# First attention of a two-layer block: key tiles taken two at a time, in phases, on TensorE

## The chip, the cores and the metric

One Trainium2 chip, one of its cores. The number is the device time of one execution in microseconds (us), the median of several. Five engines of the core work at once, each through its own list of instructions, in order, and wait for one another by semaphores: TensorE (PE, matrix products; its weight loads are listed apart as PEld), VectorE (DVE), ScalarE (ACT), GpSimd (POOL), and SyncE (SP), which here only issues DMAs.

## What is computed

Sequence of 2048 tokens of 128 features, two layers; each sub-layer is followed by a residual addition and a layer norm. The change touches the first sub-layer alone, causal attention with 16 heads of 64:

```python
q = jnp.einsum('bpm,hmd->bphd', x, Q_w) + Q_b          # k, v alike
logits = jnp.einsum('bqhd,bkhd->bhqk', q, k) / math.sqrt(D_HEAD)
logits = jnp.where(causal, NEG_MASK, logits)            # keys after the query
scores = jax.nn.softmax(logits, axis=-1)
attn = jnp.einsum('bhqk,bkhd->bqhd', scores, v)
return jnp.einsum('bqhd,hdm->bqm', attn, O_w) + O_b
```

Behind it come a gated feed-forward network, a second attention with 16 heads of 8, and a linear layer. They are the same in both kernels.

## The kernel before

**Units and turns.** Two heads are worked together, one in partitions 0 to 63, one in 64 to 127. A unit `u` is one such pair of heads (`p`, eight of them) and one block of 512 queries (`qc`, four of them), 32 units in all. A turn is one unit and one tile of 128 keys (`kt`); a unit has 4, 8, 12 or 16 turns, a pair of heads 40, the whole 320. The last four turns of a unit lie on the diagonal: they compute 512, 384, 256 and 128 queries (512, 512, 256 and 128 in a unit with `qc` 0).

**A turn on TensorE.** `scores` makes the transposed logits of both heads in `ps_e` (two slots of two banks, by the parity of the turn): three products per head of float16 parts (line 491, 64 rows of the array each, the two heads in the two halves of it), on the diagonal a mask product on 128 rows (L496, L497), and a product with two rows that subtracts the row maximum (`maxima`, L512). The maxima of an even turn come last in its slot; those of the odd turn behind it are issued right behind them as the first write of the other slot, so that the four stand together. ScalarE takes the exponential (`exps`, L383) into one of six buffers `probs`; TensorE multiplies it with the values into `ps_o` (`pv`, L527, float32, each head in 64 columns of the array); GpSimd adds the same buffers up to the row sums (L348, L353).

**Maximum blocks.** The row maxima are needed ahead of a unit. For later units, some 20 turns ahead, TensorE makes the logits of 128 queries against up to 512 keys in `ps_x`, one slot of two banks (`max_block`, L443, on 64 rows; a block on the diagonal gets a mask product, L447, on 128 rows), and VectorE reduces them (`take_max`, L592). The next block waits until that reduction is done (`s_xf`). There are 320 blocks, nearly always one per turn, in the order `u`, `t` (query tile), `c` (block of keys). Behind a unit's last block VectorE joins its parts and splits them into two bfloat16 rows (`split_max`, L601 to L605), TensorE transposes them (`mt`, L456), and SyncE copies them with four small DMAs to `mrow`, for which the unit's maxima wait (`s_mrd`).

**Ring work.** One bank `ps_y` serves, at most once per turn, at the turn's end and strictly in order, the operations that `plan` lays out: projections of q and k of the next pair of heads (`qk`, L425; ScalarE empties the bank with L400, then VectorE with L619), its values (`v`, L429; ScalarE, L407), and for each finished unit the sum over partitions (`sum`, L465; VectorE, L623), its spread (`bc`, L470; VectorE, L627) and the output projection (`yo`, L472; VectorE, L635). Each waits until the one before it has been emptied (`s_yf`). 208 of 320 turns have one.

**Order.** TensorE per turn: `scores`, first maximum block, `pv` of the turn before, other maximum blocks, ring operation. VectorE per turn: reduction of the blocks, then its part of the ring operation. ScalarE per turn: exponential, at a unit's first turn the copy of `ps_o` of the unit before (L390), its part of the ring operation. A turn's products wait for the exponential of two turns before (`s_ex`), and the first turn of a unit for `s_mrd` ahead of its products.

Of the kernel before, what the change touches and what calls it, by code (L numbers as in the profile page):

```python
# [14 lines left out]
P = 128  # L15
# [4 lines left out]
NQ = S // QC  # L20
H0, D0 = 16, 64
# [119 lines left out]
def build(nc, a, out):  # L141
# [10 lines left out]
    with ExitStack() as ctx:  # L152
# [82 lines left out]
        def diag(qc, kt):  # L235
            return kt - 4 * qc if kt >= 4 * qc else None

        def off(qc, kt):

            j = diag(qc, kt)  # L240
            return 0 if j is None or kt < 2 else P * j

        BLOCKS = [(u, t, c) for u in range(NU) for t in range(4) for c in range(u % NQ + 1)]
# [113 lines left out]
        def _(act):  # L357
# [52 lines left out]
            for turn, (u, kt) in enumerate(TURNS):  # L410
                exps(turn)
                if kt == 0 and u > 0:
                    copy_pv(u - 1)
                for op in PLAN[turn][1]:
                    empty(op)
# [3 lines left out]
        def _(pe):  # L419
# [13 lines left out]
            def max_block(n, b):  # L433
                u, t, c = BLOCKS[b]
                p, qc = divmod(u, NQ)
                w = width(b)
                if n:
                    pe.wait_ge(s_xf, n)
                if p > 0 and b == BEND[u - 1] and qc == 0:
                    pe.wait_ge(s_yf, AT["qk", 8 * p + 7] + 1)  # L440
                for h in range(2):
                    rows = slice(D0 * h, D0 * h + D0)
                    mm = pe.matmul(ps_x[:, h, 0:w], hi["q"][rows, p % 2, (4 * qc + t) * P:(4 * qc + t + 1) * P],  # L443
                                   hi["k"][rows, p % 2, c * QC:c * QC + w], start=True, stop=c < qc)
                if c == qc:
                    for h in range(2):
                        mm = pe.matmul(ps_x[:, h, w - P:w], identb[:, :], mask[:, :], start=False, stop=True)  # L447
                mm.then_inc(s_xp, 1)
# [26 lines left out]
            def scores(turn):  # L475
                u, kt = TURNS[turn]
                p, qc = divmod(u, NQ)
                o = off(qc, kt)
                keys = slice(kt * P, (kt + 1) * P)
                queries = slice(qc * QC + o, (qc + 1) * QC)  # L480
                out = ps_e[:, turn % 2]
                j = diag(qc, kt)
                if kt == 0:
                    pe.wait_ge(s_mrd[u % 4], 64 * (u // 4 + 1))
                if turn >= 2 and turn % 2 == 0:
                    pe.wait_ge(s_ex, turn - 1)
                products = ((hi, hi), (hi, lo), (lo, hi))
                for n, (k_part, q_part) in enumerate(products):
                    for h in range(2):
                        rows = slice(D0 * h, D0 * h + D0)  # L490
                        mm = pe.matmul(out[:, h, o:], k_part["k"][rows, p % 2, keys], q_part["q"][rows, p % 2, queries],  # L491
                                       start=n == 0 and turn % 2 == 0, stop=n == 2 and j is None and turn % 2 == 1)
                if j is not None:
                    for h in range(2):
                        for b in range(o // P, j):
                            pe.matmul(out[:, h, b * P:(b + 1) * P], allneg[:, :], identb[:, :], start=False, stop=False)  # L496
                        mm = pe.matmul(out[:, h, j * P:(j + 1) * P], mask[:, :], identb[:, :], start=False,  # L497
                                       stop=turn % 2 == 1)
                if turn % 2 == 0:
                    mm = maxima(turn, 0)  # L500
                mm.then_inc(s_st, 1)
                if turn % 2 == 0:
                    if turn >= 1:
                        pe.wait_ge(s_ex, turn)
                    maxima(turn + 1, 1)

            def maxima(turn, first):
                u, kt = TURNS[turn]
                o = off(u % NQ, kt)
                for h in range(2):  # L510
                    row = 64 * h + 32 * first
                    mm = pe.matmul(ps_e[:, turn % 2, h, o:], negone[row:row + 2, :], mrow[row:row + 2, u % 4, o:],  # L512
                                   start=first == 1, stop=first == 0)
                return mm
# [38 lines left out]
            for b in range(BEND[0]):  # L553
                max_block(b, b)
# [4 lines left out]
            for turn, (xs, ys) in enumerate(PLAN):  # L559
                scores(turn)  # L560
                for b in xs[:1]:
                    max_block(b, b)
                if turn > 0:
                    pv(turn - 1)
                for b in xs[1:]:
                    max_block(b, b)
                for op in ys:
                    use_y(op)
# [5 lines left out]
        def _(dve):  # L574
# [71 lines left out]
            for xs, ys in PLAN:  # L646
                for b in xs:
                    take_max(b, b)
                for op in ys:
                    empty(op)  # L650
# [875 lines left out]
```

## Time and profile before

| | us |
|---|---|
| median of 3 runs | 2081.2 (2079.88 to 2084.37) |
| profiled execution, time | 2082.02 |
| its span in the trace | 2080.3 |
| first attention, turns 0 to 319 and tail | from 36 to 952 |
| TensorE granted clock, mean | 0.933 |

The profile is of one execution; times in it count from the start of the span. An engine is busy while one of its instructions is in flight. TensorE's products are pipelined, so what one costs is read as the distance from its start to the start of the next, and not from its duration, which contains the time through the array. "PEclk" is the granted TensorE clock as a share of 2.4 GHz; 0.50 is the lower of its two levels, 1.2 GHz.

### The profile page before, as it was taken

The page shows a single profiled execution, that of the slowest core. Times are in us where ns is not written, and L with a number is a line of the kernel's source. Part 1 is how long each engine was busy: PE and PEld are TensorE (multiplying, and loading weights), DVE is VectorE, ACT ScalarE, POOL GpSimd, SP SyncE. Part 2 cuts the span into 40 slices and gives each one's busy share as a digit, 9 for nine tenths or more (in the row PEclk, how much of TensorE's full clock was granted, in tenths as well). Part 3 has the DMA queues.
Part 4 walks back from the last instruction along what each step waited for, and adds up shares of the span by engine and source line. Part 5 has one row for each costly group of instructions (what it writes and reads, how often), then busy time and mean ns, then how long its engine had stood idle before and what let it go on. Part 6 is the DMA issues. An engine that isn't in the chain of part 4 may idle for free. (4 is left out here: it accounts for less than half of the span.)

```text
span 2080.3 us, 27643 instructions
## 1 busy us (share of the span) xinstructions
PE 1738.2 (84%) x11088; PEld 559.5 (27%) x11088; DVE 1288.8 (62%) x1810; ACT 940.1 (45%) x1087; POOL 596.3 (29%) x313
## 2 busy tenths in 40 slices
PE   5889999999999999994999503788888888888873
PEld 2233333333333333323444300111111111111111
DVE  3545555564655555524200785888888888888816
ACT  2334443444434444341311300477777777677760
POOL 0357576757575756681000300000000000000000
PEclk8899999999999999995999755799999999999996
DMA  3000000000000000001000145011110021110000
GB/s 61 1 1 1 1 1 1 2 1 2 1 1 1 2 1 1 1 1 56 0 0 0 17 171 98 1 21 40 35 21 20 20 43 32 21 20 20 2 3 23
DMA packets 47714, 39.03 MB, mean 19 GB/s; under 512 B 19519, under 2 KB 42595, under 8 KB 47587
## 3 DMA queue, kind: packets, MB, share of 16 engines
q1 hardware_dynamic: 41394, 35.71, 7.6%
q10 hardware_dynamic: 6192, 1.57, 0.5%
q8 instruction: 87, 1.43, 0.3%
q14 instruction: 41, 0.33, 0.0%
HBM read 25.53 MB, written 10.49 MB: 17 GB/s over the span
## 5 line engine op out<-in xcount | busy, mean ns | idle before, releaser
L1214 ACT ACTIVATE probs<-ps_e 128x1024 f32<-128x1024 f32 x512 | 498.1, 1022 | 256.9 <-PE ps_e L1275 256.8
L353 POOL TENSOR_TENSOR acc<-acc,probs 128x1024 f32<-128x1024 f32 (+3 forms) x256 | 502.2, 1962 | 174.4 <-ACT probs L383 161.7
L592 DVE TENSOR_REDUCE maxpart<-ps_x 128x2 f32<-128x1024 f32 (+2 forms) x320 | 340.4, 1064 | 240.9 <-PE ps_x L447 121.5
L383 ACT ACTIVATE probs<-ps_e 128x1024 f32<-128x1024 f32 (+1 forms) x320 | 288.6, 902 | 426.5 <-PE ps_e L512 257.5
L1335 DVE TENSOR_REDUCE maxpart<-ps_x 128x2 f32<-128x1024 f32 x351 | 428.1, 1220 | 66.8 <-PE ps_x L1239 64.0
L527 PE MATMUL ps_o<-probs,v 128*64 128x512 f32 (+3 forms) x1280 | 309.0, 561 | 0.6 <-ACT pv_raw L390 0.6
L1285 PE MATMUL ps_o<-probs,v 128*9 128x512 f32 x2048 | 269.2, 598 | 46.5 <-ACT probs L1214 30.8
L1239 PE MATMUL ps_x<-krows,qrows 60*128 60x512 bf16 x702 | 152.7, 402 | 144.3 <-DMA qrows<-g_rows 72.2
L1339 DVE TENSOR_REDUCE maxpart<-ps_y 128x1 f32<-128x512 f32 x322 | 220.4, 685 | 18.8 <-PE ps_y L1239 15.9
L1275 PE MATMUL ps_e<-qrows,krows 62*128 62x512 bf16 x1024 | 220.6, 384 | 7.4 <-DMA qrows<-maxrow 3.7
L1239 PE MATMUL ps_y<-krows,qrows 60*128 60x512 bf16 x322 | 129.2, 401 | 7.8
L443 PE MATMUL ps_x<-k_hi,q_hi 64*128 64x512 f16 (+3 forms) x640 | 116.7, 361 | 18.6 <-DVE maxpart L592 16.9
L348 POOL TENSOR_TENSOR acc<-probs 128x1024 f32<-128x1024 f32 x32 | 75.1, 2348 | 190.2 <-ACT probs L383 190.2
L491 PE MATMUL ps_e<-q_hi,k_hi 64*128 64x512 f16 (+3 forms) x640 | 116.1, 360 | 10.7 <-DMA mrow<-maxrow 10.7
L1239 PEld LDWEIGHTS ps_x<-krows,qrows 60*128 60x128 bf16 x702 | 36.2, 94 | 302.9 <-DVE maxpart L1335 212.9
L491 PE MATMUL ps_e<-q_lo,k_hi 64*128 64x512 f16 (+3 forms) x640 | 112.8, 349 | 0.0
L491 PE MATMUL ps_e<-q_hi,k_lo 64*128 64x512 f16 (+3 forms) x640 | 112.7, 349 | 0.0
L1275 PEld LDWEIGHTS ps_e<-qrows,krows 62*128 62x128 bf16 x1024 | 58.9, 95 | 101.1 <-ACT probs L1214 73.0
L527 PEld LDWEIGHTS ps_o<-probs,v 128*64 128x64 f32 x1280 | 63.7, 135 | 64.7 <-issue 50.4
L791 DVE SCALAR_TENSOR_TENSOR yt<-ps_f,sc_w,xt 128x512 f32<-128x512 f32 x4 | 3.0, 751 | 121.7 <-PE ps_f L748 121.7
L491 PEld LDWEIGHTS ps_e<-q_hi,k_hi 64*128 64x128 f16 x640 | 30.8, 93 | 166.8 <-issue 119.8
L1239 PEld LDWEIGHTS ps_y<-krows,qrows 60*128 60x128 bf16 x322 | 30.5, 95 | 134.2 <-DVE maxpart L1339 105.5
(222 smaller groups left out, 1531.0 us busy)
## 6 DMA issues: line engine op xcount, KB each, us to landing
qrows<-q_rows SPq DMA_DIRECT2D x64, 192.0 KB
k_rows<-parts_k SPq DMA_DIRECT2D x6, 512.0 KB
q_rows<-parts_q SPq DMA_DIRECT2D x6, 512.0 KB
krows<-k_rows SPq DMA_DIRECT2D x8, 384.0 KB, 7.2
qrows<-g_rows SPq DMA_DIRECT2D x64, 48.0 KB
mrow<-maxrow SPq DMA_DIRECT2D x128, 2.0 KB
raw_h<-in_L_ffn_h_w SPq DMA_DIRECT2D x2, 1024.0 KB, 7.1
g_rows<-parts_a SPq DMA_DIRECT2D x6, 256.0 KB
```

What stands on the lines that cost most here:

```text
L353: pool.tensor_tensor(acc[:, u % 2, :, o:], acc[:, u % 2, :, o:], probs[:, turn % RING, :, o:], ALU.add)\
L383: act.activation(probs[:, turn % RING, :, o:], ps_e[:, turn % 2, :, o:], ACT.Exp, scale=1.0 / math.sqrt(D0))\
L443: mm = pe.matmul(ps_x[:, h, 0:w], hi["q"][rows, p % 2, (4 * qc + t) * P:(4 * qc + t + 1) * P], hi["k"][rows, p % 2, c * QC:c * QC + w], st ...
L491: mm = pe.matmul(out[:, h, o:], k_part["k"][rows, p % 2, keys], q_part["q"][rows, p % 2, queries], start=n == 0 and turn % 2 == 0, stop=n ...
L527: mm = pe.matmul(ps_o[D0 * h:D0 * h + D0, o:], v[:, p % 2, kt, D0 * h:D0 * h + D0], probs[:, turn % RING, h, o:], start=kt == 0, stop=kt = ...
L592: dve.reduce_max(maxpart[:, u % 2, :, t, c:c + 1], ps_x[:, :, 0:width(b)], AX.X).then_inc(s_xf, 1)
L1214: act.activation(probs[:, HG * (turn % 2) + hh], ps_e[:, e % 2], ACT.Exp).then_inc(s_ex, 1)
L1239: return pe.matmul(out, qrows[64 * j:64 * j + R_M, u % 3, c, hh, t * P:(t + 1) * P], krows[64 * j:64 * j + R_M, u // NQ % 2, hh, c * KB:(c ...
L1275: mm = pe.matmul(ps_e[:, e % 2, j], krows[64 * j:64 * j + R_END, u // NQ % 2, hh, at * P:(at + 1) * P], qrows[64 * j:64 * j + R_END, u % 3 ...
L1285: mm = pe.matmul(ps_o[32 * hh:32 * hh + D1 + 1, :], v1[:, TU * j + at, HG * (u // NQ) + hh, :], probs[:, HG * (turn % 2) + hh, j, :], star ...
L1335: dve.reduce_max(maxpart[:, at:at + op[2]], ps_x[:, 0:op[2], :], AX.X).then_inc(s_xf, 1)
L1339: dve.reduce_max(maxpart[:, at:at + 1], ps_y[:, :], AX.X).then_inc(s_yf, 1)
```

## The change

Two turns are taken together. TensorE: first maximum block of the two (with its mask), products of both turns, products of the second maximum block, masks of both turns, mask of the second block, maxima of both turns, `pv` of the turn two before, any further blocks and the first turn's ring operation, then `pv` of the turn one before and the second turn's ring operation. ScalarE: both exponentials, then the copy of `ps_o`, then both ring parts. VectorE: the reductions of both turns' blocks, then both ring parts. The order of the blocks within a unit now alternates a full block with a diagonal one as long as there are diagonal ones. The wait for `s_mrd` stands ahead of the maxima, no longer ahead of the products. Numbers and sizes of all instructions stay the same; GpSimd and SyncE are as they were.

```diff
--- before.py
+++ after.py
@@ -240,7 +240,15 @@
             j = diag(qc, kt)
             return 0 if j is None or kt < 2 else P * j
 
-        BLOCKS = [(u, t, c) for u in range(NU) for t in range(4) for c in range(u % NQ + 1)]
+        def unit_blocks(u):
+
+            qc = u % NQ
+            full = [(u, t, c) for t in range(4) for c in range(qc)]
+            last = [(u, t, qc) for t in range(4)]
+            mixed = [b for two in zip(full, last) for b in two]
+            return mixed + full[4:] if full else last
+
+        BLOCKS = [b for u in range(NU) for b in unit_blocks(u)]
         BEND = [sum(4 * (w % NQ + 1) for w in range(u + 1)) for u in range(NU)]
 
         def width(b):
@@ -407,12 +415,15 @@
                     act.activation(v[:, p % 2, 4 * g:4 * g + 4, :].rearrange("p t d -> p (t d)"), ps_y[:, :], ACT.Copy)\
                         .then_inc(s_yf, 1)
 
-            for turn, (u, kt) in enumerate(TURNS):
+            for turn in range(0, len(TURNS), 2):
+                u, kt = TURNS[turn]
                 exps(turn)
+                exps(turn + 1)
                 if kt == 0 and u > 0:
                     copy_pv(u - 1)
-                for op in PLAN[turn][1]:
-                    empty(op)
+                for t in (turn, turn + 1):
+                    for op in PLAN[t][1]:
+                        empty(op)
             copy_pv(NU - 1)
 
         @block.tensor
@@ -430,22 +441,32 @@
                                    wv[:, 2 * p:2 * p + 2, :].rearrange("m h d -> m (h d)"), start=True, stop=True)
                 return mm
 
-            def max_block(n, b):
+            def max_products(b):
                 u, t, c = BLOCKS[b]
                 p, qc = divmod(u, NQ)
                 w = width(b)
-                if n:
-                    pe.wait_ge(s_xf, n)
+                if b:
+                    pe.wait_ge(s_xf, b)
                 if p > 0 and b == BEND[u - 1] and qc == 0:
                     pe.wait_ge(s_yf, AT["qk", 8 * p + 7] + 1)
                 for h in range(2):
                     rows = slice(D0 * h, D0 * h + D0)
                     mm = pe.matmul(ps_x[:, h, 0:w], hi["q"][rows, p % 2, (4 * qc + t) * P:(4 * qc + t + 1) * P],
                                    hi["k"][rows, p % 2, c * QC:c * QC + w], start=True, stop=c < qc)
-                if c == qc:
+                if c < qc:
+                    mm.then_inc(s_xp, 1)
+
+            def max_mask(b):
+                u, t, c = BLOCKS[b]
+                w = width(b)
+                if c == u % NQ:
                     for h in range(2):
                         mm = pe.matmul(ps_x[:, h, w - P:w], identb[:, :], mask[:, :], start=False, stop=True)
-                mm.then_inc(s_xp, 1)
+                    mm.then_inc(s_xp, 1)
+
+            def max_block(b):
+                max_products(b)
+                max_mask(b)
 
             def use_y(op):
                 kind, i, n = op
@@ -472,46 +493,40 @@
-            def scores(turn):
+            def products(turn):
                 u, kt = TURNS[turn]
                 p, qc = divmod(u, NQ)
                 o = off(qc, kt)
                 keys = slice(kt * P, (kt + 1) * P)
                 queries = slice(qc * QC + o, (qc + 1) * QC)
-                out = ps_e[:, turn % 2]
-                j = diag(qc, kt)
+                if turn >= 2:
+                    pe.wait_ge(s_ex, turn - 1)
+                for n, (k_part, q_part) in enumerate(((hi, hi), (hi, lo), (lo, hi))):
+                    for h in range(2):
+                        rows = slice(D0 * h, D0 * h + D0)
+                        pe.matmul(ps_e[:, turn % 2, h, o:], k_part["k"][rows, p % 2, keys],
+                                  q_part["q"][rows, p % 2, queries], start=n == 0, stop=False)
+
+            def score_masks(turn):
+                u, kt = TURNS[turn]
+                o, j = off(u % NQ, kt), diag(u % NQ, kt)
+                if j is not None:
+                    for h in range(2):
+                        out = ps_e[:, turn % 2, h]
+                        for b in range(o // P, j):
+                            pe.matmul(out[:, b * P:(b + 1) * P], allneg[:, :], identb[:, :], start=False, stop=False)
+                        pe.matmul(out[:, j * P:(j + 1) * P], mask[:, :], identb[:, :], start=False, stop=False)
+
+            def maxima(turn):
+                u, kt = TURNS[turn]
+                o = off(u % NQ, kt)
                 if kt == 0:
                     pe.wait_ge(s_mrd[u % 4], 64 * (u // 4 + 1))
-                if turn >= 2 and turn % 2 == 0:
-                    pe.wait_ge(s_ex, turn - 1)
-                products = ((hi, hi), (hi, lo), (lo, hi))
-                for n, (k_part, q_part) in enumerate(products):
-                    for h in range(2):
-                        rows = slice(D0 * h, D0 * h + D0)
-                        mm = pe.matmul(out[:, h, o:], k_part["k"][rows, p % 2, keys], q_part["q"][rows, p % 2, queries],
-                                       start=n == 0 and turn % 2 == 0, stop=n == 2 and j is None and turn % 2 == 1)
-                if j is not None:
-                    for h in range(2):
-                        for b in range(o // P, j):
-                            pe.matmul(out[:, h, b * P:(b + 1) * P], allneg[:, :], identb[:, :], start=False, stop=False)
-                        mm = pe.matmul(out[:, h, j * P:(j + 1) * P], mask[:, :], identb[:, :], start=False,
-                                       stop=turn % 2 == 1)
-                if turn % 2 == 0:
-                    mm = maxima(turn, 0)
+                for h in range(2):
+                    row = 64 * h + 32 * (turn % 2)
+                    mm = pe.matmul(ps_e[:, turn % 2, h, o:], negone[row:row + 2, :], mrow[row:row + 2, u % 4, o:],
+                                   start=False, stop=True)
                 mm.then_inc(s_st, 1)
-                if turn % 2 == 0:
-                    if turn >= 1:
-                        pe.wait_ge(s_ex, turn)
-                    maxima(turn + 1, 1)
-
-            def maxima(turn, first):
-                u, kt = TURNS[turn]
-                o = off(u % NQ, kt)
-                for h in range(2):
-                    row = 64 * h + 32 * first
-                    mm = pe.matmul(ps_e[:, turn % 2, h, o:], negone[row:row + 2, :], mrow[row:row + 2, u % 4, o:],
-                                   start=first == 1, stop=first == 0)
-                return mm
 
             def pv(turn):
                 u, kt = TURNS[turn]
@@ -551,21 +566,35 @@
             pe.wait_ge(s_cst, 12)
             pe.wait_ge(s_cstv, 1)
             for b in range(BEND[0]):
-                max_block(b, b)
+                max_block(b)
             for op in BEFORE:
                 use_y(op)
             pe.wait_ge(s_pjv, 4)
             pe.wait_ge(s_ob, 2)
-            for turn, (xs, ys) in enumerate(PLAN):
-                scores(turn)
+            for turn in range(0, len(TURNS), 2):
+                two = (turn, turn + 1)
+                xs = [b for t in two for b in PLAN[t][0]]
                 for b in xs[:1]:
-                    max_block(b, b)
-                if turn > 0:
-                    pv(turn - 1)
-                for b in xs[1:]:
-                    max_block(b, b)
-                for op in ys:
-                    use_y(op)
+                    max_block(b)
+                for t in two:
+                    products(t)
+                for b in xs[1:2]:
+                    max_products(b)
+                for t in two:
+                    score_masks(t)
+                for b in xs[1:2]:
+                    max_mask(b)
+                for t in two:
+                    maxima(t)
+                for t in two:
+                    if turn > 0:
+                        pv(t - 2)
+                    if t == turn:
+                        for b in xs[2:]:
+                            max_block(b)
+                    for op in PLAN[t][1]:
+                        use_y(op)
+            pv(len(TURNS) - 2)
             pv(len(TURNS) - 1)
             for op in AFTER:
                 use_y(op)
@@ -643,11 +672,13 @@
             dve.wait_ge(s_ob, 2)
             dve.wait_ge(s_xtc, 4)
             dve.tensor_scalar(yt[:, :], xt[:, :], obias[:, 0:1], None, ALU.add).then_inc(s_yi, 1)
-            for xs, ys in PLAN:
+            for turn in range(0, len(TURNS), 2):
+                xs = [b for t in (turn, turn + 1) for b in PLAN[t][0]]
                 for b in xs:
                     take_max(b, b)
-                for op in ys:
-                    empty(op)
+                for t in (turn, turn + 1):
+                    for op in PLAN[t][1]:
+                        empty(op)
             for op in AFTER:
                 empty(op)
             dve.wait_ge(s_yf, len(AT))
```

## Rows read from the trace of the kernel before

**Rows 1.** The page's first part, busy time of each engine

```profile
PE 1738.2 (84%) x11088; PEld 559.5 (27%) x11088; DVE 1288.8 (62%) x1810; ACT 940.1 (45%) x1087; POOL 596.3 (29%) x313
```

**Rows 2.** Windows: stretch, length, busy us by engine, granted clock, DMA share, GB/s

```profile
36.00:147.00 111.00, 90.09 (x533) 29.97 (x533) 56.41 (x70) 30.25 (x38) 40.09 (x21) 0.82 0.00 1
705.00:816.00 111.00, 110.69 (x784) 38.92 (x782) 62.55 (x77) 45.93 (x57) 72.16 (x36) 1.00 0.01 1
1500.00:1900.00 400.00, 331.86 (x2360) 72.74 (x2356) 355.96 (x433) 284.99 (x298) 0.00 (x0) 1.00 0.13 27
```

**Rows 3.** Timeline, VectorE: one event in three successive pairs of heads

```profile
499.86 1.59 DVE L603 CAST maxhl<-rowmax 128x8 bf16<-128x8 f32 x1
...
610.65 1.59 DVE L603 CAST maxhl<-rowmax 128x8 bf16<-128x8 f32 x1
...
721.43 1.59 DVE L603 CAST maxhl<-rowmax 128x8 bf16<-128x8 f32 x1
```

**Rows 4.** Timeline, TensorE, from 703.40: start, duration, engine, line, out<-in, count

```profile
703.40 0.39 PE L491 MATMUL ps_e<-q_hi,k_hi 64*128 64x512 f16 x2
...
704.15 0.39 PE L512 MATMUL ps_e<-mrow,negone 2*128 2x512 bf16 x4
704.48 0.39 PE L443 MATMUL ps_x<-k_hi,q_hi 64*128 64x512 f16 x2
704.80 1.08 PE L527 MATMUL ps_o<-probs,v 128*64 128x512 f32 x4
705.81 0.39 PE L491 MATMUL ps_e<-q_hi,k_hi 64*128 64x512 f16 x2
...
706.47 0.27 PE L443 MATMUL ps_x<-k_hi,q_hi 64*128 64x256 f16 x2
706.67 0.28 PE L447 MATMUL ps_x<-mask,identb 128*128 128x128 bf16 x2
706.89 1.08 PE L527 MATMUL ps_o<-probs,v 128*64 128x512 f32 x4
707.90 0.64 PE L465 MATMUL ps_y<-acc,ones 128*32 128x128 f32 x16
708.48 0.39 PE L491 MATMUL ps_e<-q_hi,k_hi 64*128 64x512 f16 x2
```

**Rows 5.** Timeline, VectorE: a reciprocal behind the sum at 707.90

```profile
708.61 0.96 DVE L623 RECIPROCAL rden<-ps_y 128x128 f32<-128x128 f32 x1 [0.92 <-PE ps_y L465]
```

**Rows 6.** Timeline, 723 to 725: a block that waited for VectorE

```profile
723.14 1.22 DVE L592 TENSOR_REDUCE maxpart<-ps_x 128x2 f32<-128x1024 f32 x1
724.42 0.39 PE L443 MATMUL ps_x<-k_hi,q_hi 64*128 64x512 f16 x2
724.85 1.23 DVE L592 TENSOR_REDUCE maxpart<-ps_x 128x2 f32<-128x1024 f32 x1 [0.37 <-PE ps_x L443]
```

**Rows 7.** Timeline, 641 to 645: a projection and what empties it

```profile
641.99 1.12 PE L425 MATMUL ps_y<-xt,wq 128*128 128x512 f32 x2
643.05 0.39 PE L491 MATMUL ps_e<-q_hi,k_hi 64*128 64x512 f16 x2
643.16 0.69 ACT L400 ACTIVATE q_hi<-ps_y,bq 128x512 f16<-128x512 f32 x1 [1.48 <-PE ps_y L425]
643.88 0.75 DVE L619 SCALAR_TENSOR_TENSOR q_lo<-ps_y,bq,q_hi 128x512 f16<-128x512 f32 x1 [1.55 <-ACT q_hi L400]
644.57 1.23 DVE L592 TENSOR_REDUCE maxpart<-ps_x 128x2 f32<-128x1024 f32 x1
```

**Rows 8.** Groups by line and form: count, busy us, mean ns, idle before

```profile
L383 ACT ACTIVATE probs<-ps_e 128x1024 f32<-128x1024 f32 x232 | 237.7, 1025 | 335.9 <-PE ps_e L512 223.4 <-PE ps_e L491 100.8 <-PE ps_e L497 9.6
L353 POOL TENSOR_TENSOR acc<-acc,probs 128x1024 f32<-128x1024 f32 x168 | 395.0, 2351 | 118.6 <-ACT probs L383 111.4 <-POOL acc L353 0.4
L627 DVE TENSOR_TENSOR ctxn<-pv_raw,ps_y 128x512 f32<-128x512 f32 x32 | 22.0, 688 | 29.2 <-PE ps_y L470 29.2
L390 ACT ACTIVATE pv_raw<-ps_o 128x512 f32<-128x512 f32 x32 | 18.9, 592 | 0.7 <-PE ps_o L527 0.7
```

**Rows 9.** Timeline, TensorE: the two waits for mrow ahead of clock drops

```profile
60.72 0.39 PE L491 MATMUL ps_e<-q_hi,k_hi 64*128 64x512 f16 x2 [1.78 <-DMA mrow<-maxrow]
63.91 0.64 PE L491 MATMUL ps_e<-q_hi,k_hi 64*128 64x512 f16 x2
136.47 0.39 PE L491 MATMUL ps_e<-q_hi,k_hi 64*128 64x512 f16 x2 [2.86 <-DMA mrow<-maxrow]
```

**Rows 10.** Windows around the second of those waits

```profile
137.00:147.00 10.00, 6.84 (x38) 3.23 (x34) 5.04 (x8) 1.62 (x2) 0.00 (x0) 0.52 0.01 2
```


## The prediction

> **What bounds the kernel now.** I read the page's first part, then windows over the attention, then TensorE's timeline in it. Over the span TensorE is in flight 84% of the time [rows 1]; in the attention it is in flight 110.69 of 111 us at a granted clock of 1.00, VectorE 62.55, ScalarE 45.93, GpSimd 72.16 [rows 2]. So TensorE's issue sets the time from about 147 us on, and each microsecond taken from its stream, or in which it waits, shows in the end. The first 111 us are different: 90.09 in flight, clock 0.82. A pair of heads, 40 turns, repeats every 110.8 us (one event recurs at 499.86, 610.65 and 721.43) [rows 3].
>
> The timeline gives each group's price as distance between starts [rows 4]. Products of a turn: 0.66 if another group on 64 rows follows (705.81 to 706.47), 0.75 if one on two rows follows (703.40 to 704.15). The four maxima to the block 0.33, a full block to `pv` 0.32; at 512 columns one pass of two halves is 0.66/3 = 0.22. A block of 256 to its mask 0.20, the mask's pair to `pv` 0.22, `pv` 1.01, the sum 0.58. In each place where the use of the array changes (64 rows, two rows, 128 rows, 64 columns) about 0.10 is paid: 0.75 - 0.66, 0.33 - 0.22, 0.32 - 0.22.
>
> **What the change takes away.** No instruction is removed; their neighbours change. From the two orders in the code I counted the places per 40 turns where the use of the array changes: 188 before, 122 after. Behind a `pv` there were 40 of them and are 34: 6 of the 66 lie there, where another `pv` follows, a neighbourhood that these rows do not show. Its price is between 4 x 0.22 = 0.87 (no seam at all) and 1.01 (nothing saved); I take 0.96, that of two halves, and the bounds are worth 0.5 us per 40 turns. So TensorE's stream loses 60 x 0.10 + 6 x 0.05 = 6.3, and goes from 110.8 less 0.6 of waits to 103.9 us per 40 turns.
>
> The Trainium skill (TensorEngine Tiling, Key Properties) says that changing the tiling mode drains the engine; by it all 66 places would save alike, 6.6 in place of 6.3. The same page (PSUM Bottleneck) says that tiling speeds TensorE up and not the emptying of PSUM: a rule against this change. The next part finds the same from rows.
>
> **What it adds: waits for VectorE.** A pair of turns now begins with a block X0, then come two turns of products, then a second block X1 in the same single slot `ps_x`. X1 waits for the reduction of X0, and all of TensorE behind it. In the before a `pv` (1.01) and a turn's products (0.66, or 0.75 and 0.33 of maxima) lay between two blocks, 2.0 us from start to start or more. Price of the loop: block start to reduction start 0.43 (724.42 to 724.85), the full reduction 1.23, and 0.06 from its end to the next block (723.14 + 1.22 = 724.36, block at 724.42) [rows 6]: 1.72. Cover now: X0 0.22 and two products of 0.66, 1.54. So even the undisturbed pair waits 0.18. Where the turns are 512 and 384 wide the cover is 0.16 shorter, wait 0.34; at 256 and 128 (0.34 and 0.18 in place of 1.32) it is 0.98.
>
> Worse: VectorE takes its work in order, and in front of X0's reduction lies its part of the ring operation that TensorE issued just before X0. Before, that had a whole turn's products as cover.
> - `qk`: TensorE start 641.99, next group at 643.05, ScalarE 643.16 to 643.85, VectorE from 643.88, and the reduction queued behind it starts at 644.57 [rows 7], 1.52 after the next group. Now X0 is that next group: reduction done at 1.52 + 1.23 + 0.06 = 2.81 against a cover of 1.54: wait 1.26.
> - `sum`: issued at 707.90, next group 708.48 [rows 4], reciprocal from 708.61 for 0.96, to 709.57 [rows 5]. The reduction starts about 1.0 after X0 in place of 0.43: wait 0.74.
> - `bc` and `yo`: TensorE's group is some 1.07 long, VectorE needs 0.69 behind it [rows 8]: 0.30 later than free, wait 0.48.
> - `v` has no VectorE part: 0.18 again.
>
> In the plan `qk` is due on odd turns, so 5 of 8 end a pair. I laid the changed order of 40 turns (120 to 159, units 12 to 15) on these prices, engine by engine. Of the 20 pairs 5 wait 0.18 (0.9), 1 waits 0.34, 1 0.98, 1 0.61 (a masked 384-wide X0 before narrow turns), 3 behind `sum` 0.74, 0.74 and 1.54 (narrow), 3 behind `bc` or `yo` 0.48, 5 behind `qk`: 1.26, 1.26, 1.42, 1.52 and, before narrow turns, 2.53. Together 0.9 + 1.9 + 3.0 + 1.4 + 8.0 = 15.2.
>
> **Ring operations closer together.** When both turns of a pair have one, only one `pv` lies between them. A `qk` in the even turn must be emptied by ScalarE, which now has two exponentials of 1.03 first and sometimes the copy of `ps_o` (0.59) [rows 8], then by VectorE. The second waits four times in these 40 turns: 2.16 (behind a 128-wide `pv`), 0.84, 0.63, 0.11, sum 3.7.
>
> Net per 40 turns: -6.3 - 0.6 (the old waits, among them) + 15.2 + 3.7 = +12.0 us.
>
> **Other edits.** Products wait for the exponential two turns before: two exponentials in a row need 2.1 us behind the maxima, and two `pv` (1.97), X0 and the first products (0.66) stand ahead of the second one's slot; cost nothing, at narrow `pv` at most 0.3 once per unit. If that cover went, it would cost 0.4 to 0.7 per pair. GpSimd's add takes 2.35 [rows 8], a pair of full turns some 5.5; six buffers hold that. SP's DMAs keep their work, and the `mrow` wait moves behind 1.3 us of products: it held TensorE 1.78 and 2.86 at 60.72 and 136.47 [rows 9], so 1 to 3 us come back in all.
>
> **The sum.** Against the profiled execution's 2082.0 (span 2080.3): turns 0 to 39, where few `qk` stand behind narrow turns and the `mrow` waits shrink, -2.5 (bounds -7 to +5: they are bound by blocks already); turns 40 to 279, six pairs of heads, 6 x 12.0 = +72; turns 280 to 319 have no `qk` and no `v` of a next pair, 7 to 8 of waits against 6 saved, +2. That is +71.5, 2153.5. The same laying of the old order gives 915 us for the attention where the trace has 916, so the prices are sound.
>
> **The clock.** After the `mrow` waits of 1.78 and 2.86 the granted clock fell to its lower level: products at 63.91 take 0.64 in place of 0.39, and 137 to 147 shows 0.52 [rows 9, 10]. Later, 1500 to 1900, TensorE is in flight 83% of the time and keeps 1.00 [rows 2]. The changed attention would be around 85%, but with single waits of 2.5 and 2.2 us once per 40 turns, near those that were followed by a fall. I expect some eight falls of 7 to 10 us in the attention that weren't there. All of the first 111 us, at 0.82, lose only 5 or 6 us against the same laying at full clock, since other waits hide it; so I take +1 per fall, +8, bounds 0 and 3.4 each (half of a 7 us stretch), 0 to 27. **2161** on the median, which is 0.8 below the profiled time.
>
> **Rivals.**
> - *The waits are covered* (other side): TensorE's X1 finds the reduction done, since VectorE's ring parts end early enough. It decides if a reduction is done within 1.54 of X0. Then 6.3 per 40 turns are left, 8 x 6.5 = 52: 2030. Against it: 1.72 is measured and is over 1.54 with nothing in front. 0.05.
> - *Half of it*: half the waits, as VectorE is less late than laid. Per 40 turns 0.5 x 18.9 - 6.9 = +2.6, 6 x 2.6 = +16: 2097. For it: the few waits of before for this slot were 0.2 each. 0.05. Down to no change at all: 0.02.
> - *The seams don't shrink*: 0.10 is paid for whatever follows, also between two products or two `pv`. Then 50 more, 2205. Against: 0.66 and 0.75 differ only by the neighbour. 0.04.
> - *The clock falls often*: each pair of heads has 3 or 4 falls at 2 to 3 us each, +60 more: 2200. For it: the 19 waits per 40 turns; against: 83% at 1.00 [rows 2]. 0.09. [...]
> - Forecast: the remaining 0.75.
>
> The range takes the forecast with its bounds (2161 less 27 for the size of waits and falls, with a fifth of the waits on either side, 6 x 3.8 = 23) and part of the two upper rivals: 2122 to 2195. A change under 0.2% (4 us) can't be told from none. Faster 0.05, same 0.02, slower 0.93.
>
> **What the profile after would show.** Right: in 40 turns, about 123 us in place of 110.8; PE or PEld idle before L443's counterpart, released by `maxpart`, 14 to 16 us per 40 turns, in single waits of 0.2 to 2.5; products to second block 1.32 plus the wait; `pv` behind maxima; waits of ring operations for ScalarE or VectorE; VectorE's busy time unchanged, with less idle per reduction waiting for TensorE's maxima; the attention ending near 1025 to 1030. Wrong: TensorE still in flight 99% of the attention; or idle before L443 under 5 us per 40 turns; or idle before the products, released by `probs`; or a clock under 0.9 over 200 to 900.

## The result and the profile after

The changed kernel takes 2167.3 us (2166.84 to 2169.73) against 2082.8 for the kernel before measured beside it: ratio 1.041, 95% interval 1.0392 to 1.0428, slower. Predicted were 2161 us and a range of 2122 to 2195. The profiled execution took 2167.78 us with a span of 2166.1.

The page's first part of the changed kernel, to be read against [rows 1]:

```profile
PE 1714.9 (79%) x11088; PEld 582.4 (27%) x11088; DVE 1308.0 (60%) x1810; ACT 921.7 (43%) x1087; POOL 596.0 (28%) x313
```

Same counts on every engine, but TensorE is in flight for a smaller share of a longer span. Windows of the changed kernel over the attention (columns as in [rows 2]):

```profile
36.00:147.00 111.00, 85.48 (x562) 31.87 (x558) 58.84 (x73) 32.05 (x42) 42.85 (x23) 0.88 0.00 1
250.00:850.00 600.00, 520.19 (x3767) 201.17 (x3764) 310.86 (x365) 206.66 (x268) 347.38 (x174) 0.97 0.01 1
```

520 of 600 us in flight, where the kernel before had 110.69 of 111, and a granted clock of 0.97 in place of 1.00: two losses. Of the first, the waits in the same window say what it is (waiting engine, line, released by: us in total, times, longest):

```profile
PEld ps_x L454 <- DVE maxpart L621: 99.0, 94, 2.5
...
PE ps_x L454 <- DVE maxpart L621: 59.1, 69, 2.3
```

L454 is the product of a maximum block, L621 VectorE's reduction. The weight load and the product of one wait are counted apart, so these are not to be added.

How often a pair of heads repeats is read from an event that recurs, as in [rows 3]:

```profile
376.97 2.31 DVE L632 CAST maxhl<-rowmax 128x8 bf16<-128x8 f32 x1
...
503.21 2.32 DVE L632 CAST maxhl<-rowmax 128x8 bf16<-128x8 f32 x1
...
629.34 2.31 DVE L632 CAST maxhl<-rowmax 128x8 bf16<-128x8 f32 x1
```

126.2 us against 110.8. In what follows "per 40 turns" is this period, or the distance from the products of turn 40 to those of turn 280, divided by six (126.5 in the changed kernel, since the first of the six periods is 1.7 longer). The span grew by 85.8, made up of: turns 40 to 279 +94.3 (759.0 against 664.7), the 40 before -2.0, the 38 behind -1.9, what lies ahead of the attention -2.8, what follows it -1.9.

The worst single wait, on the timeline: a projection (L436) stands in front of a pair of narrow turns. Some rows of ScalarE and VectorE between are kept:

```profile
437.42 1.12 PE L436 MATMUL ps_y<-xt,wk 128*128 128x512 f32 x2
438.47 0.39 PE L454 MATMUL ps_x<-k_hi,q_hi 64*128 64x512 f16 x2
438.55 0.61 ACT L398 ACTIVATE pv_raw<-ps_o 128x512 f32<-128x512 f32 x1
...
439.02 0.70 ACT L408 ACTIVATE k_hi<-ps_y,bk 128x512 f16<-128x512 f32 x1
...
439.14 0.22 PE L507 MATMUL ps_e<-q_hi,k_lo 64*128 64x128 f16 x2
439.75 0.75 DVE L648 SCALAR_TENSOR_TENSOR k_lo<-ps_y,bk,k_hi 128x512 f16<-128x512 f32 x1 [2.57 <-ACT k_hi L408]
440.42 1.22 DVE L621 TENSOR_REDUCE maxpart<-ps_x 128x2 f32<-128x1024 f32 x1
441.69 0.61 PE L454 MATMUL ps_x<-k_hi,q_hi 64*128 64x512 f16 x2 [2.34 <-DVE maxpart L621]
...
443.10 3.68 PE L542 MATMUL ps_o<-probs,v 128*64 128x512 f32 x8
```

X0 is issued at 438.47. Its reduction starts at 440.42, for VectorE first has to finish the projection, and that waits for ScalarE, which copies `ps_o` first. X1 gets through 0.05 after the reduction, at 441.69. And its product now takes 0.61 in place of 0.39: the granted clock has gone to its lower level, and two `pv` are in flight for 3.68. At full clock, earlier in the same kernel, two `pv` look like this:

```profile
427.60 1.94 PE L542 MATMUL ps_o<-probs,v 128*64 128x512 f32 x8
429.47 0.39 PE L454 MATMUL ps_x<-k_hi,q_hi 64*128 64x512 f16 x2
```

From start to start 1.87 for both, where 1.97 had been taken (0.96 and 1.01 [rows 4]). The merged line hides the second start; in the trace it comes 0.91 after the first, and the next group 0.96 after that.

### The profile page after: what moved, and what is told of

Its sections match the earlier page's. It is cut to its first block and busy times, and to the rows that moved or that the text cites. A ratio compares the mean times of both kernels' runs of the same rounds, so it can differ in the third digit from the quotient of the medians.

```text
span 2166.1 us, 27612 instructions
## 1 busy us (share of the span) xinstructions
PE 1714.9 (79%) x11088; PEld 582.4 (27%) x11088; DVE 1308.0 (60%) x1810; ACT 921.7 (43%) x1087; POOL 596.0 (28%) x313
## 5 line engine op out<-in xcount | busy, mean ns | idle before, releaser
L391 ACT ACTIVATE probs<-ps_e 128x1024 f32<-128x1024 f32 (+1 forms) x320 | 270.9, 898 | 565.0 <-PE ps_e L527 565.0
L621 DVE TENSOR_REDUCE maxpart<-ps_x 128x2 f32<-128x1024 f32 (+2 forms) x320 | 338.9, 1059 | 201.5 <-PE ps_x L464 106.5
L542 PE MATMUL ps_o<-probs,v 128*64 128x512 f32 (+3 forms) x1280 | 303.6, 568 | 0.0
L454 PE MATMUL ps_x<-k_hi,q_hi 64*128 64x512 f16 (+3 forms) x640 | 119.5, 370 | 103.9 <-DVE maxpart L621 102.6
L454 PEld LDWEIGHTS ps_x<-k_hi,q_hi 64*128 64x128 f16 x640 | 31.2, 94 | 250.6 <-DVE maxpart L621 175.6
L542 PEld LDWEIGHTS ps_o<-probs,v 128*64 128x64 f32 x1280 | 69.8, 138 | 100.0 <-issue 63.3
L652 DVE RECIPROCAL rden<-ps_y 128x128 f32<-128x128 f32 x32 | 30.6, 957 | 73.7 <-PE ps_y L486 73.7
```

Of the source, the lines that this page charges most:

```text
L391: act.activation(probs[:, turn % RING, :, o:], ps_e[:, turn % 2, :, o:], ACT.Exp, scale=1.0 / math.sqrt(D0))\
L542: mm = pe.matmul(ps_o[D0 * h:D0 * h + D0, o:], v[:, p % 2, kt, D0 * h:D0 * h + D0], probs[:, turn % RING, h, o:], start=kt == 0, stop=kt = ...
L621: dve.reduce_max(maxpart[:, u % 2, :, t, c:c + 1], ps_x[:, :, 0:width(b)], AX.X).then_inc(s_xf, 1)
```

## Experiments

Two theories to begin with. A: the loss is X1's wait for the reduction of X0 in the single slot `ps_x`, made longer by what stands in front of it on VectorE. B: the loss comes from ring operations that stand closer together and from the paired exponentials, and the blocks only show it.

**e1: the second block behind the first `pv`.**

```diff
-                for b in xs[1:2]:
-                    max_products(b)
                 for t in two:
                     score_masks(t)
-                for b in xs[1:2]:
-                    max_mask(b)
...
                     if turn > 0:
                         pv(t - 2)
                     if t == turn:
-                        for b in xs[2:]:
+                        for b in xs[1:]:
                             max_block(b)
```

> The changed kernel with one move: the second maximum block of a pair (products and mask) is issued behind the first pv, no longer behind the products. Between X0 and X1 there are then 0.22 + 1.32 + 0.33 + 0.86 = 2.7 us and more, over the 1.72 that the slot needs, at narrow turns about 1.6. Theory A (the time lost is X1's wait for the reduction of X0 in the one slot): waits before blocks fall from 15 us to about 4 per 40 turns, those of ring operations stay at 4 to 5, 40 turns take about 113 us in place of 126; total 2104, range 2092 to 2115. Theory B (the time is lost to ring operations that stand too close together and to the paired exponentials; blocks only show it): under 3 us per 40 turns change hands, total 2145 or more.

Measured: 2092.8 us, ratio 1.0048 (1.0031 to 1.0064); 40 turns take 112.5 us. Waits from 250 to 850 us, and under them one row of the changed kernel in the same window:

```profile
PE ps_y L493 <- DVE k_lo L644: 10.3, 5, 2.1
...
PE ps_x L454 <- DVE maxpart L617: 4.3, 10, 0.5
```

```profile
PE ps_y L493 <- DVE k_lo L648: 8.2, 4, 2.1
```

Products that waited for the slot: 59.1 us became 4.3. The wait of the output projection (L493) for a `k_lo` in front of it, 2.1 each, is still there, as it is in the changed kernel. Moving this one block gives back 75 of 85 us, at the lower end of A's range: A holds. The 75 hold more than the wait itself, since from turn 40 to 280 the clock fell twice in place of eleven times. What ring operations cost is the next experiment.

**e2: blocks and ring operations both spread over the pair.** On TensorE:

```diff
-                for b in xs[:1]:
-                    max_block(b)
                 for t in two:
                     products(t)
-                for b in xs[1:2]:
+                for b in xs[:1]:
                     max_products(b)
...
-                for b in xs[1:2]:
+                for b in xs[:1]:
                     max_mask(b)
+                for op in PLAN[turn][1]:
+                    use_y(op)
                 for t in two:
                     maxima(t)
-                for t in two:
...
+                if turn > 0:
+                    pv(turn - 2)
+                for b in xs[1:2]:
+                    max_block(b)
+                if turn > 0:
+                    pv(turn - 1)
+                for b in xs[2:]:
+                    max_block(b)
+                for op in PLAN[turn + 1][1]:
+                    use_y(op)
```

ScalarE empties the first ring operation ahead of both exponentials; VectorE takes block, ring part, block, ring part.

> Blocks and ring operations both spread over the pair: TensorE does products of both turns, first block, masks, first ring operation, maxima, first pv, second block, second pv, second ring operation; ScalarE empties the first ring operation ahead of the two exponentials; VectorE takes block, ring, block, ring. Theory A, with ring operations as second term: 40 turns take about 107 us (before 110.8, changed 126.2), no single wait over 1.7 us from turn 40 on and so no falls of the clock there; total 2046, range 2038 to 2056, faster than both. Theory B (the paired exponentials or seams that aren't saved bound it): 2085 or more, with idle time before products released by probs.

Measured: 2042.1 us, ratio 0.9807 (0.9792 to 0.9822), inside A's range, faster than the kernel before by 41 us and than the changed one by 125; 40 turns take 106.7 us, and the clock did not fall between turns 40 and 280. Window and waits:

```profile
250.00:850.00 600.00, 594.83 (x4430) 226.31 (x4430) 340.59 (x425) 240.94 (x312) 408.39 (x205) 1.00 0.01 1
```

```profile
PEld ps_x L455 <- DVE maxpart L624: 47.1, 59, 1.2
...
PE ps_x L455 <- DVE maxpart L624: 4.7, 16, 0.4
...
PE ps_e L508 <- ACT probs L391: 0.3, 1, 0.3
```

The 47 us of the weight load are hidden under products in flight (TensorE is in flight 594.83 of 600); products waited 4.7 us. The paired exponentials cost 0.3 us in 600. So B falls as the main cause; what it says of ring operations is the second term: e1 takes 112.0 in a period without a fall, 5.3 more than e2, at nearly the same number of changes of use. Pairing turns does save TensorE time, but e2 has other neighbours than the changed kernel. Counted in the traces, turns 120 to 159, the use of the array changes 187 times in the kernel before, 122 times in the changed one, 146 times in e2 and 148 times in e1. The 41 fewer of e2 (187 less 146) at 0.10 are 4.1 us, and 110.8 less 106.7 is 4.1.

**e3: the changed kernel with short reductions.**

```diff
-                dve.reduce_max(maxpart[:, u % 2, :, t, c:c + 1], ps_x[:, :, 0:width(b)], AX.X).then_inc(s_xf, 1)
+                dve.reduce_max(maxpart[:, u % 2, :, t, c:c + 1], ps_x[:, :, 0:P], AX.X).then_inc(s_xf, 1)
```

> The changed kernel, but VectorE's reduction of a block reads the first 128 of its columns only (the maxima over the other keys are left out); 0.43 us in place of up to 1.23. TensorE's stream is the same. Theory A: waits before blocks fall from 15 to about 4 us per 40 turns (what is left is VectorE's ring part queued in front), 40 turns take 112 us plus some 4 for the clock; total 2087, range 2078 to 2098. Theory B: waits of ring operations and of the clock stay and the time stays over 2140.

Measured: 2063.9 us; 112.6 us per 40 turns. Waits from 250 to 850 us:

```profile
PE ps_x L454 <- DVE maxpart L621: 17.6, 30, 1.5
PE ps_y L493 <- DVE k_lo L648: 10.3, 5, 2.1
```

The direction is A's, and so is the wait before blocks, 59.1 down to 17.6. The total is below A's range by 14: most of the 4 us per 40 turns set aside for the clock were not needed, although the clock fell once in each of the six periods, for 3.4 us.

**e4: the changed kernel with the projections one turn later.**

```diff
-                    due.setdefault(TP * (p - 1) + 1 + 2 * i, []).append(("qk", 8 * p + i))
+                    due.setdefault(TP * (p - 1) + 2 + 2 * i, []).append(("qk", 8 * p + i))
```

> The changed kernel, with the projections of q and k due one turn later, on even turns, so that a pv lies between most of them and the next first block. Waits per 40 turns: 16 in place of 19, and the single waits over 1.7 us behind turn 40 go from 13 to 1. If the falls of the clock come from the longest single waits, they go too, and with them 20 to 24 us: total 2131, range 2122 to 2145. If the falls come from the sum of waits, they stay: 2150 to 2160.

Measured: 2144.1 us, 120.8 per 40 turns, at the upper end of the first range. Window and waits of 250 to 850:

```profile
250.00:850.00 600.00, 530.68 (x3902) 203.91 (x3902) 323.37 (x377) 215.96 (x277) 358.43 (x179) 1.00 0.01 1
```

```profile
PEld ps_x L454 <- DVE maxpart L621: 90.8, 105, 1.6
...
PE ps_x L454 <- DVE maxpart L621: 46.7, 70, 1.3
```

The sum of waits at weight loads is nearly that of the changed kernel (90.8 against 99.0), at products it is 46.7 against 59.1. The longest before a block is 1.6 in place of 2.5. No product waited over 1.4 for anything, and no fall of the clock is left: 1.00. This speaks for long single waits as what brings the lower clock here, and against their sum, which the second expectation named.

**e5 and e6: waits put into the kernel before.** Does one long wait do it anywhere?

```diff
+                for n_ in range(3 if u % NQ == 3 and t == 2 and c == 0 else 0):
+                    dve.reduce_max(spare[:, n_, :], ps_x[:, :, 0:width(b)], AX.X)
                 dve.reduce_max(maxpart[:, u % 2, :, t, c:c + 1], ps_x[:, :, 0:width(b)], AX.X).then_inc(s_xf, 1)
```

e6 has one repetition, ahead of each of four blocks (`c == 0`).

> The kernel before, with three idle repetitions of one reduction on VectorE (1.23 us each) ahead of one block per pair of heads, eight places in all. By the prices of the rows each makes TensorE wait 2.5 us there and 0.35 a little later, 21 to 23 us in all. Theory F1 (a single wait of 2.5 us brings the lower clock, wherever it stands): seven or eight falls behind turn 40, at 2 to 3 us each, total 2120 to 2125. Theory F2 (the fall needs other waits close by, as in the changed kernel; TensorE's stream of before is dense): none to two falls, total 2104 to 2106.

> The kernel before, with one idle repetition of a reduction (1.23 us) ahead of four blocks per pair of heads. By the prices one wait of 1.4 us and one of 0.4 per pair of heads, 14 us in all. Both theories: no fall of the clock behind turn 40; total 2097, range 2094 to 2101.

Measured: e5 2118.4 us, between its theories; 114.3 per 40 turns. Its wait of 2.54 stands once in each of the six periods between turns 40 and 280. The clock fell behind three of the six, every other one, for 3.4 us each. One of them, on TensorE's timeline:

```profile
460.29 0.39 PE L444 MATMUL ps_x<-k_hi,q_hi 64*128 64x512 f16 x2 [2.54 <-DVE maxpart L595]
460.61 1.08 PE L528 MATMUL ps_o<-probs,v 128*64 128x512 f32 x4
461.62 1.97 PE L473 MATMUL ps_y<-ctxn,wo 128*128 128x512 f32 x2
463.52 0.61 PE L492 MATMUL ps_e<-q_hi,k_hi 64*128 64x512 f16 x2
```

The output projection takes 1.90 in place of 1.06. e6, with single waits of at most 1.2 before the product, took 2100.7 us, in its range (112.9 per 40 turns), and had one fall between turns 40 and 280, where none was expected, at 202 us; the kernel before has none there. So a wait of 2.5 us was followed by a fall three times in six even in a dense stream, one of 1.2 once in six. Neither F1 nor F2 is right as stated. The total of e5 is 12 over F2's range: besides the falls, the turns before 40 took 6.3 us more than in the kernel before, and turns 280 to 318 took 7.2 more.

The length of a wait does not settle it alone. The changed kernel, e8 and e9 (below) have the same twelve long waits between turns 40 and 280, six of 2.3 and six of 2.1 us at a product, and eleven, five and three falls. e3 and e1 both have six of 2.1, and six and two falls. The sum does not settle it either: between turns 40 and 280 the products of e3 waited 42 us in all, with six falls, those of e4 83 us, with none. What else decides, no run here shows.

**e7: e2 with the old order of blocks.** `BLOCKS` as in the kernel before.

> The kernel e2 with the order of blocks within a unit as in the kernel before. The seams and the slot's distances stay nearly as they are: same time as e2, 2042, within 3 us. If alternating full with diagonal blocks is what made room for the slot, 2050 or more.

Measured: 2042.2 us, ratio 0.9806 (0.9789 to 0.9822), 106.7 us per 40 turns: the alternation of full and diagonal blocks does nothing in this arrangement. In the changed kernel itself it was not tried.

**e8 and e9: the cast of eight columns.** Comparing the changed kernel's pairs of turns with the laid order one by one, two per 40 turns were too long without a fall of the clock: turns 138 and 139 took 9.06 us where 7.8 had been laid, 152 and 153 5.38 for 4.6. In the first stands this (GpSimd, VectorE, TensorE):

```profile
503.15 4.84 POOL L361 TENSOR_TENSOR acc<-acc,probs 128x1024 f32<-128x1024 f32 x2 [2.37 <-ACT probs L391]
503.21 2.32 DVE L632 CAST maxhl<-rowmax 128x8 bf16<-128x8 f32 x1
...
505.64 0.68 DVE L656 TENSOR_TENSOR ctxn<-pv_raw,ps_y 128x512 f32<-128x512 f32 x1
506.38 1.12 PE L493 MATMUL ps_y<-ctxn,wo 128*128 128x512 f32 x2 [1.27 <-DVE ctxn L656]
```

The cast of eight columns starts 0.06 us after the first of two GpSimd adds, which the line merges, and ends with that add, 2.3 us later; TensorE waits 1.27 for what is queued behind it. In the kernel before, 14 of 32 casts began while a GpSimd add was running; all 14 took 1.56 to 1.59 [rows 3], the other 18 took 0.17. There it cost TensorE nothing: no wait of its products from turn 40 to 280 was over 0.1 us.

e8 gives GpSimd almost nothing to do:

```diff
-                    pool.tensor_tensor(acc[:, u % 2, :, o:], acc[:, u % 2, :, o:], probs[:, turn % RING, :, o:], ALU.add)\
+                    pool.tensor_tensor(acc[:, u % 2, :, o:o + 8], acc[:, u % 2, :, o:o + 8], probs[:, turn % RING, :, o:o + 8], ALU.add)\
```

> The changed kernel with GpSimd's adds of the third and later key tiles over 8 columns in place of up to 512 per head (most of the row sums is left out), so that GpSimd is nearly idle. Theory C (VectorE's cast of 8 columns, 2.3 us twice per pair of heads against 0.17 at best, is held for as long as a GpSimd add runs): every cast takes 0.17, pairs 138 and 152 of the timeline come down from 9.06 and 5.38 to 7.8 and 4.6 us, 40 turns from 126.2 to about 124, total 2154, range 2148 to 2160. If the cast is slow for another reason, the total stays at 2167.

e9 does without the cast:

```diff
-                dve.wait_ge(s_rm, 2 * u + 1)
-                dve.tensor_copy(maxhl[:, :, 0, :], rowmax[:, :, :]).then_inc(s_rm, 1)
+                dve.reduce_max(maxhl[:, :, 0, :], maxpart[:, u % 2, :, :, 0:u % NQ + 1], AX.X).then_inc(s_rm, 1)
```

> The changed kernel with the cast replaced by a second reduction straight into bfloat16. Theory C1 (GpSimd's add holds every small VectorE operation that reads a second SBUF input too): the wait moves to the subtraction behind it, which reads two, and that takes up to 2.3 us; total 2165 to 2169, as the changed kernel. Theory C2 (the cast alone is held): both are short and the total is 2150 to 2158.

Measured: e8 2138.8 us, ratio 1.0265 (1.0248 to 1.0282). The cast's line of e8 (minimum, median, maximum in ns), and under it that of the subtraction in e9:

```profile
L632 DVE CAST maxhl<-rowmax x32: 170/172/207, 32.2 to 965.0; 128x8 bf16<-128x8 f32 x32
```

```profile
L633 DVE TENSOR_TENSOR maxhl<-rowmax,maxhl x32: 166/958/2267, 32.4 to 975.0; 128x8 bf16<-128x8 f32 x32
```

With GpSimd idle no cast is over 0.21, and the two pairs take 7.73 and 4.59 us, as laid. The total is 9 under C's range. In e9 the reduction that replaces the cast takes 0.16, and the subtraction behind it, with two inputs from SBUF, takes up to 2.27: the wait moved, as C1 said. All 28 subtractions that began during a GpSimd add ended with it. No reduction of this size took over 0.19, with an add running or not. The total of e9 is 2160.3 (ratio 1.0371, interval 1.0351 to 1.0391), some 5 under C1's range, with three falls of the clock from turn 40 on in place of eleven; C2's 2150 to 2158 is missed too, and the duration of the subtraction decides against it. Without falls of the clock a period of e9 takes 123.1, 1.7 more than one of e8. The Trainium skill (VectorE: DVE Perf Modes, Two Vector instructions with no wait between them) states that a second SBUF read interface is shared with GpSimd; the rows of the subtraction agree with it and show what it costs. The cast has one input; why it is held too, no run shows.

e8 came out 15 us below its centre: it has five falls of the clock in place of eleven, for a reason that stays open, and what follows the attention took 6 us less. A period of it without a fall takes 121.4 us, with one 123.1, with two 124.15. That prices a fall at 1.0 to 1.7 us; in e5 one costs 1.6.

## Why the prediction was right

**Direction and mechanism** held, and the size: 2161 forecast, 2167.3 measured, +79 forecast against +84.6. That the size is this close is partly luck, as the terms below show: the waits and seams were laid 8 us too dear, two other terms were 13 and 10 us too small, and the ends of the attention and the stages around it gave back 8 that were not forecast. The rows that decided were [rows 6] (1.72 for the slot's loop) against two products and a block (1.54), and [rows 7] (what VectorE has queued in front behind a projection). e1 and e3 show that wait, and e2 shows that the pairing as such costs nothing. As listed are TensorE in flight 87%, waits released by `maxpart` in single ones of up to 2.5 and the maxima in front of `pv`. Not as listed: the last VectorE step of the attention ends at 1043 (1025 to 1030 was named), and VectorE's busy time is not unchanged but 19 us more, 16 of them in the casts. The 14 to 16 us of idle time per 40 turns before blocks are 12.4 at products and 20.8 at weight loads as the profile counts them.

**The terms, per 40 turns.** Laid were 6.3 saved in seams, 15.2 of waits before blocks and 3.7 of ring waits, +12.0 net. A period without casts held and without falls is that of e8, 121.4, +10.6. The two waits were laid right. In turns 120 to 159 of e8 the second blocks start 15.0 us later, added up, than the spacing of the products in front of them would have it, the six longest 2.50, 1.51, 1.40, 1.39, 1.24 and 1.24, where 2.53, 1.54, 1.52, 1.42, 1.26 and 1.26 had been laid. Its ring operations waited 2.1, 0.8, 0.6 and 0.1, together 3.6. So 0.3 of the 1.4 lie in waits. Up to 0.6 lie in seams: two `pv` take 1.87 and not 1.97, in six places. The rest is not taken apart. At six periods the 1.4 are 8 us.

**A term that was missing:** casts held by GpSimd, 1.3 + 0.8 = 2.1 per 40 turns (9.06 - 7.73 and 5.38 - 4.59), 13 us in all. e9 puts the held subtraction that takes its place at 1.7. The rows of the kernel before showed the long cast (1.59 in [rows 3]), and the prediction has no term for it. It cost nothing there, with TensorE in flight 110.69 of 111 [rows 2]; it came to count when X1 and the ring operations began to wait for VectorE.

**A term that was too small:** the clock. The mechanism, a fall behind the longest single waits, held: ten of the eleven falls between turns 40 and 280, of 3.4 or 6.8 us each, came with a wait of 2.1 or 2.3, and none came in e4. Forecast were eight falls of 7 to 10 us at +1. The full period is 126.2 = 121.4 + 2.1 + 2.7, and 2.7 is also what two falls cost in e8 (124.15 - 121.4). With a third fall in the first period that is 18 us, over twice the +8. How many falls the waits bring was not foreseeable from the rows: e8 and e9, with the same long waits, have five and three. The low rate of the first 111 us (5 to 6 us lost at 0.82) was a poor guide; it was read from a stretch in which TensorE waits for blocks anyway.

**Small ones.** Turns 0 to 39: -2.0 against -2.5, which is chance: the changed kernel has one stretch at the lower clock there, 10.2 us, the kernel before four, together 27. The last 38 turns: -1.9 against +2 for the last 40. The stages around the attention, which were taken as unchanged, gave 4.7 us back. The cause is not known, but what follows turn 318 is nearly all the same code in all runs, and it took from 1134.9 to 1147.7 us in the eleven profiled executions, so 4.7 is within what they vary by. Experiments are best compared by their 40 turns.

**The rivals.** *Covered* needed a reduction within 1.54 us, and in turns 120 to 159 of e8 only one of the 20 second blocks, behind a block of 128 columns, finds it done. *Half of it* fell with the 15.0 and 3.6. *The seams don't shrink* fell: two `pv` take 1.87, and e2, with 41 fewer changes of use, saves the 4.1 us per 40 turns that 0.10 each gives. *The clock falls often* was right in kind, with one or two falls per period (three in the first) and not three or four, and under a third of its +60.

**Slips in its sums.** 50 on top of 2161 is 2211, where 2205 stands for the seams; 60 is 2221, where 2200 stands for the clock; and 2161 less 27 and 23 is 2111, where the range begins at 2122. None of them bears on the result.

## What to carry to other kernels

When work is moved together into phases, count for each single-slot buffer what now lies between its two uses, and compare it with write, emptying and hand-over as one loop; then ask what the emptying engine has queued in front of it at that moment. Saving seams (places where the use of the array changes) is worth something only if the steps that need another engine's answer stay apart: spreading them between the phases turned a kernel 4.1% slower into one 1.9% faster, though over a third of the saved seams came back with it. Price an instruction at its slowest row as well as at its median before it comes to lie on a path.

## What was not expected of the hardware

- A VectorE cast of 8 columns takes 0.17 us, or up to 2.34 if it begins while a GpSimd add is running; it then ends with the add. A two-input subtraction of the same size takes up to 2.27 (e9). A reduction of the same size is not held (0.16 to 0.19).
- After a single wait of 2.5 us in an otherwise full stream TensorE's granted clock went to its lower level three times in six (e5), and once in six after one of 1.2 (e6). With 83 us of waits at products between turns 40 and 280, none over 1.4, it stayed at its higher level (e4).
- Two float32 `pv` on 64 columns, at 512 columns of data, take 1.87 us one behind the other (0.91 and 0.96), and 1.01 each when another use of the array follows each.
